# The scratch of the convolution's cells, laid out with two phases side by side

## The reference

```
x = x + L0(gn(x))     # shifted 8x8 window mixing, 16 heads
x = x + L1(gn(x))     # linear attention over two scales

qkv  = w_qkv @ x                        # 768 channels
y    = conv5x5(qkv, depthwise) ; y = conv1x1(y, 96 groups of 8)
mqkv = concat(qkv, y)                   # 64 heads of 3 x 8 channels
q, k = relu(...), relu(...) ; v with a row of ones
vk   = v k^T  (8+1 x 8 per head and image)
out  = (vk q)[:8] / (vk q)[8]           # then w_proj and a batch norm
```

## Time and profile before

| | |
|---|---|
| three runs | 2719.42, 2726.9, 2731.26 us |
| profiled execution | 2727.02 us, span 2725.0 us |
| PE, DVE, ACT, POOL busy | 94%, 75%, 57%, 39% of the span |
| mean granted clock of TensorE | 0.983 |
| DMA | 285,099 packets, 628.32 MB, mean 231 GB/s |
| stores of cells | 384 of 408 KB, landing 3.9 us after issue (median) |
| loads of raw | 192 of 816 KB, 6.3 us |

### The profile page before, as it was taken

The page is one execution under the profiler, slowest core; times in us unless marked ns, Lnnn a source line. Parts: engine busy times, 40 slices in busy tenths (PEclk is TensorE's granted clock), DMA queues, the critical chain, the costliest instruction groups (busy, mean ns, idle before and its releaser), DMA issues. The chain is left out here.

```text
span 2725.0 us, 59098 instructions
## 1 busy us (share of the span) xinstructions
PE 2559.2 (94%) x20989; PEld 2015.3 (74%) x20989; DVE 2057.2 (75%) x2947; ACT 1565.7 (57%) x2137; POOL 1062.9 (39%) x1364
## 2 busy tenths in 40 slices
PE   4999998999999999959999999999999969999997
PEld 3777776777777777748888888888888836666665
DVE  4667666788778778758888888888888758888884
ACT  4666654666656666646666666666666623434342
POOL 6300003777777768840000000000000028888886
PEclk9999999999999999979999999999999979999999
DMA  5453526888878887898888888888888667887772
GB/s 167 182 213 146 201 86 209 303 301 325 318 286 292 317 291 285 273 276 204 201 200 199 201 200 201 199 201 200 200 199 201 169 217 260 288 289 275 262 262 124
DMA packets 285099, 628.32 MB, mean 231 GB/s; under 512 B 35184, under 2 KB 232560, under 8 KB 279280
## 3 DMA queue, kind: packets, MB, share of 16 engines
q1 hardware_dynamic: 274256, 561.69, 67.3%
q0 software_dynamic: 7936, 38.80, 4.2%
q10 hardware_dynamic: 2720, 25.43, 2.5%
HBM read 328.05 MB, written 300.94 MB: 231 GB/s over the span
## 5 line engine op out<-in xcount | busy, mean ns | idle before, releaser
L1687 POOL TENSOR_TENSOR ql<-q,qh 128x1024 fp32r<-128x1024 f32 x128 | 305.9, 2420 | 1034.2 <-ACT qh L1715 1034.2
L1360 PE MATMUL c_ps<-dh,wh 128*128 128x512 f32 x1152 | 471.9, 410 | 21.4 <-DVE wl L1470 19.1
L1268 ACT ACTIVATE dh<-raw 128x1632 fp32r<-128x1632 f32 x192 | 301.2, 1569 | 281.5 <-PE c_ps L1360 261.2
L1360 PE MATMUL c_ps<-dh,wl 128*128 128x512 f32 x1152 | 453.3, 394 | 0.0
L1360 PE MATMUL c_ps<-dl,wh 128*128 128x512 f32 x1152 | 452.8, 393 | 0.0
L1475 DVE TENSOR_TENSOR dl<-raw,dh 128x1632 fp32r<-128x1632 f32 x192 | 355.7, 1853 | 66.3 <-ACT dh L1268 66.3
L950 PE MATMUL o_ps<-xh,wqh 128*128 128x512 f32 x768 | 327.1, 426 | 15.7 <-DVE xl L1028 8.1
L950 PE MATMUL o_ps<-xl,wqh 128*128 128x512 f32 x768 | 303.7, 395 | 0.0
L950 PE MATMUL o_ps<-xh,wql 128*128 128x512 f32 x768 | 301.6, 393 | 0.0
L1360 PEld LDWEIGHTS c_ps<-dh,wh 128*128 128x128 f32 x1152 | 217.4, 189 | 67.7 <-issue 19.4
L1360 PEld LDWEIGHTS c_ps<-dl,wh 128*128 128x128 f32 x1152 | 216.6, 188 | 51.6
(11 more groups left out here) (211 smaller groups left out, 5431.3 us busy)
## 6 DMA issues: line engine op xcount, KB each, us to landing
qkv_scratch<-stage SPq DMA_DIRECT2D x384, 408.0 KB, 3.9
raw<-qkv_scratch SPq DMA_DIRECT2D x192, 816.0 KB, 6.3
qr_scratch<-qs SPq DMA_DIRECT2D x128, 256.0 KB, 3.0
yq_scratch<-qy SPq DMA_DIRECT2D x64, 512.0 KB, 6.8
q<-yq_scratch SPq DMA_DIRECT2D x128, 256.0 KB, 5.5
q<-qr_scratch SPq DMA_DIRECT2D x128, 256.0 KB, 6.2
ox<-x_scratch SPq DMA_DIRECT2D x8, 4096.0 KB, 14.9
out<-ox SPq DMA_DIRECT2D x8, 4096.0 KB, 13.0
```

The lines of the kernel that those rows point to most:

```text
L1268: act.activation(dh[kind][:, :], raw[kind][:, :], ACT.Copy).then_inc(hi_ready, 1)
L1360: last = pe.matmul(c_ps[:, bank(hp, j, kind, m), :], w[hp][:, kind, part, o:o + P], cells[:, :, HALF * dy:HALF * dy + HALF * NB], start=(k ...
L1687: pool.tensor_tensor(two_of(ql, n, tp), two(n, tp), two_of(qh, n, tp).bitcast(F32), ALU.subtract)\
```

## The change

The scratch becomes (3 x 32 heads, 8 pairs of phases, 8 channels, 8 images, 2, 408). The two phases of a pair are those that one unit of projections makes together (2q and 2q + 1), so they now lie beside each other for each channel and image. A store of a tile writes 3264 contiguous bytes per channel, where it wrote 1632 bytes in each of two places. A load of raw is issued as two DMAs: a = 0 fills partitions 0 to 63 with the even phases, a = 1 partitions 64 to 127 with the odd ones, each partition with four runs of 1632 bytes. ACT waits for both (32 instead of 16 on the semaphore). The rows of raw now stand in the order of even phases, then odd ones, and the taps are written to their sorted scratch in that order (line 726), in DMAs of the same shape.

```diff
--- before.py
+++ after.py
@@ -723,7 +723,8 @@
             sp.wait_ge(K["taps_out"], 16 * QT)
             for p in range(NPH):
                 src = taps_dram.rearrange("t (h c) p n -> p c (t h) n", c=D)[p, :, :, :]
-                sp.dma_start(sorted_dram[D * p:D * p + D, :, :], src).then_inc(K["taps_sorted"], 16)
+                row = D * (NPH // 2 * (p % 2) + p // 2)
+                sp.dma_start(sorted_dram[row:row + D, :, :], src).then_inc(K["taps_sorted"], 16)
             for par in range(2):
                 for g in range(GROUPS):
                     sp.wait_ge(K["x_stored"][par][g], 16 * (B // 2))
@@ -735,7 +736,7 @@
                     def tile(n, j, stored):
                         t = TILES[j]
                         p0 = 4 * ((n // 2 + 2) % 4) + 2 * ((n + 1) % 2)
-                        sp.dma_start(qkv_dram[P * t:P * t + P, p0:p0 + 2, image(i, par), :],
+                        sp.dma_start(qkv_dram[HT * t:HT * t + HT, p0 // 2, :, image(i, par), :, :].rearrange("h c a n -> h c (a n)"),
                                      stage[:, n % 2, j, :, :, :, :].rearrange("p a k y x -> p a (k y x)"))\
                             .then_inc(stored[n % 2], 16)
 
@@ -1180,7 +1181,7 @@
         summed, s_full, s_taken = sem("summed"), sem("s_full"), sem("s_taken")
         stored = [sem(f"yq_stored{i}") for i in range(2)]
 
-        qkv_v = qkv_dram.rearrange("(k h c) p b n -> k h p c (b n)", k=3, c=D)
+        qkv_v = qkv_dram.rearrange("(k h) q c b a n -> k h a (q c) b n", k=3)
         yq_v = yq_dram.rearrange("(h d) p b n -> h p d (b n)", d=D)
 
         block = ctx.enter_context(nc.Block())
@@ -1212,8 +1213,9 @@
                 sp.wait_ge(K["qr_stored"][c], 32 * 4 * B)
 
             def load(h, j, kind):
-                sp.dma_start(raw[kind][:, :], qkv_v[kind, h, :, :, IMG * PN * j:IMG * PN * j + IMG * PN])\
-                    .then_inc(raw_loaded[kind], 16)
+                for a in range(2):
+                    sp.dma_start(raw[kind][P // 2 * a:P // 2 * a + P // 2, :].rearrange("p (b n) -> p b n", b=IMG),
+                                 qkv_v[kind, h, a, :, IMG * j:IMG * j + IMG, :]).then_inc(raw_loaded[kind], 16)
 
             def store(h, j, s):
                 own.wait_ge(q_out, s + 1)
@@ -1263,7 +1265,7 @@
             def high(s, kind):
 
                 u = 3 * s + kind
-                act.wait_ge(raw_loaded[kind], 16 * (s + 1))
+                act.wait_ge(raw_loaded[kind], 32 * (s + 1))
                 at_least(act, m_full, 3 * (u - 2))
                 act.activation(dh[kind][:, :], raw[kind][:, :], ACT.Copy).then_inc(hi_ready, 1)
 
@@ -1983,7 +1985,7 @@
     out = nc.dram_tensor("out_0", (B, C, H, W), F32, kind="ExternalOutput").ap()
     scratch = {
         "x1": nc.dram_tensor("x1_scratch", (B, C, H * W), F32, kind="Internal").ap(),
-        "qkv": nc.dram_tensor("qkv_scratch", (3 * C, NPH, B, PN), F32, kind="Internal").ap(),
+        "qkv": nc.dram_tensor("qkv_scratch", (3 * AH, NPH // 2, D, B, 2, PN), F32, kind="Internal").ap(),
         "qr": nc.dram_tensor("qr_scratch", (2 * P, NPH, B, POS), F32, kind="Internal").ap(),
         "yq": nc.dram_tensor("yq_scratch", (C, NPH, B, POS), F32, kind="Internal").ap(),
         "taps_sorted": nc.dram_tensor("tap_sorted", (P, QT * HT, TAP * TAP), F32, kind="Internal").ap(),
```

## The result

The changed kernel takes 2744.6 us, the median of six runs (2732.13 to 2753.62), where the kernel before takes 2727.1 in the same session. The ratio is 1.0068, 95% interval [1.0039, 1.0098]: 17.5 us slower. That is inside the range that was given (2714 to 2755), but 17 us above the time that was named, and it is the outcome "slower by more than 14 us", which had a chance of 0.17. Timed again, it gave 2744.6 and 1.0073 [1.0051, 1.0094].

The account below looks back on a forecast made before the run. TensorE was taken to bound projections and convolution. Span 2725.0 - 2.5 (projections) + 0 (steady convolution) + 3 (convolution start) = 2725.5 us, 2727.5 with what lies around it; named 2728, range 2714 to 2755.

Parts of the forecast that it names:

- The loads' terms: Convolution: the loads cut into short runs cost 0 us in the steady part and +3 us at the start.
- The stores' term: Projections: longer store runs relieve GpSimd's wait around the image loads, -2.5 us at TensorE, bounds 0 and -10.8.
- the prediction's own list: Signs of being wrong: steady dh waiting for DMA, the store's DMA share up, or ACT's first dh unchanged at 1205.56.
- rival 1: Steady convolution: loads become the bound above 4.61 us each; at 4.8 us +36, 2764 us; chance 0.13.
- in the direction of the store the form costs nothing: Projections' stores: a 16 x 8 DRAM side is as fast as before, as the yq store has that form.
- the 131 worked out: Projections' stores: one 3264-byte run takes 13 + 118 = 131 ns, in place of 2 x 72 = 144.
- The 161 ns of a yq run: Convolution's yq store: a 4096-byte write takes 161 ns, used as evidence that the 16 x 8 form is fast.
- the third rival: Projections: the 16 x 8 form halves the stores' rate as it does the loads', +77 us, 2805; chance 0.05.
- +3 us for the start of the convolution: First raw load: its short runs alternate with GpSimd's 4096-byte runs and land 1.5 to 4.4 us later, delaying TensorE.
- about 1208: Start of the convolution: the time in the trace, in us, at which ACT's first dh should come.
- The steady convolution: Loads of 4.13 us stay hidden behind TensorE's 15.13 us step: 0 us, DMA share 0.88 to 0.90.
- the bound from above: Convolution's loads: four 1632-byte runs take at most 477 + 39 = 516 ns, the value the prediction used.

Follow-up runs that it names:

- after: The changed kernel against the kernel before, first measurement and trace: 2744.6 us, ratio 1.0068.
- again: The changed kernel measured and traced once more, nothing altered: 2744.6 us, ratio 1.0073 against the kernel before.
- st32: Kernel before with only its stores changed, to 3264-byte runs with a 32 x 4 x 816 DRAM side: 2725.4 us, ratio 0.9992.
- st128: Kernel before with only its stores changed, to 3264-byte runs in 128 equal DRAM rows: 2722.85 us, ratio 0.9992.
- mended: The changed kernel with its stores in 128 equal DRAM rows, partitions and taps reordered to match: 2722.7 us, ratio 0.9988 against the kernel before.
- ld128: Kernel before with loads of raw as 128 equal DRAM rows, taps and weights permuted, stores unchanged: 2722.2 us, ratio 0.9985.
- ld64: Kernel before with only its loads changed, to two DMAs of 64 x 4 x 408: 2725.95 us, ratio 1.0003.
- mendedg: mended with GpSimd's two loads held until the first raw lands and DVE's second taps wait moved into the loop: 2722.4 us, ratio 0.9998.
- ld128g: ld128 with GpSimd's two loads held until the first raw lands and DVE's second taps wait moved into the loop: 2718.3 us, ratio 0.9979.
- st16: Kernel before with only the changed kernel's stores, 3264-byte runs with a 16 x 8 x 816 DRAM side: 2739.2 us, ratio 1.0043.

## Where the prediction was right, and the step that failed

**The range held, the mechanism did not.** The loads' terms came out as said. The stores' term came out with the wrong sign, and by the prediction's own list this was a sign of being wrong: the stores' share of the DMA went up (and the six stretches have 16.0 us idle, where some 10 were said). That 2744.6 lies in the range is in good part luck: its upper end of 2755 was there for the loads as the bound of the convolution (rival 1), which did not come.

**The stores' term was the step that failed.** The sum had -2.5 us for the projections, bounds 0 to -10.8, resting on "in the direction of the store the form costs nothing". The traces have +5.4 and +7.2 us there (after, again), +9.8 with the stores alone. All four traces with the 16 x 8 form have projections of 751.8 to 761.8 us, the eight others 742.2 to 746.8. The terms around it held: the run costs 133 ns in the fast form against the 131 worked out, and then the stage is 3.0 to 4.2 us shorter than in the one before (st32, st128, mended). What was missing is 28 ns a run, 48 x 28 ns = 1.3 us in a unit. Against the kernel before that is 48 x (161 - 144) ns = 0.8 us more DMA time in a unit instead of 0.6 less.

**The evidence for the step was another store.** The 161 ns of a yq run were read in 1526:1527, the microsecond in which only the rest of a store is under way. Over 1300:2100 the records of the kernel before give 182 ns on the mean, and one run in ten takes 272 or more. That is not yet the form. Two thirds of these runs start with no run of a load under way and take 162 ns on the mean; the third that has one beside it takes 224. In ld128, where the loads are 128 equal rows and the yq store is untouched, all of them have 161 ns on the mean, and 2 in 100 take over 200. So the reading was right: a yq store in the 16 x 8 form runs at full speed. What failed is the step from it to the stores of cells, which have the same form, other addresses and shorter runs, and stand in a row on the queue where a yq store stands alone. There the same form costs 28 ns a run. The prediction had one case of the form slow (the loads at 477 ns) and one fast, and took direction for the difference. Direction is not it: the stores of cells are writes too.

**It was a weak form of the third rival.** That rival had the form halve the stores' rate, for 2805 us; its sign, "the store's share of the DMA up instead of down", is what came (74.6% to 80.4%). A run took a fifth longer (161 against 133 ns), not twice as long, and of the 4.5 us that TensorE lost in 452:1187, 3.0 lie in the six stretches around the images. With a chance of 0.05 and no case between nothing and half, the chance of slower was too small. The point between was open: the loads showed half, the yq store nothing, and no row had the new stores.

**The gap.** The sum had +3 us for the start of the convolution (bounds 1.5 to 4.4). ld64, with nothing else changed, gives +2.9, mended +2.8: right in size. That the competing queue is its cause is supported by the gates: holding GpSimd's transfers back shortens the gap by 5.9 us with the loads cut in four (mended, mendedg), and by 2.4 us with loads of whole rows (ld128, ld128g). The measured gap of +6.6 has a second source that the prediction did not have: the slower stores at the end of the projections; st16, whose loads are unchanged, has +7.3. By SP's timeline it is their backlog, which holds SP's last stores (issued in 3.00 us after 0.92) and with them the loads behind. The forecast of "about 1208" for ACT's first dh came to 1212.1. The two sources do not add up: +7.3 and +2.9 alone, +6.6 and +5.5 together.

**The steady convolution.** 0 us was right, PE 910 of 910, and so, closely, were the signs: share 0.87 (0.88 to 0.90 said), a load of 64 partitions landing in 5.5 us. A 1632-byte run of these loads took 120.5 ns by the records, four of them 482 where the bound from above was 516. The Trainium skill, "SBUF — State Buffer", section on the DMA port swizzle, has 64 partitions at 196 to 218 GB/s; 6528 x 16 / 482 is 217, so the trace agrees. The first rival (loads as the bound) did not come. That the load of 128 partitions was hardly faster before was not in the load's size, though, as ld128 shows.

**What this leaves of the 17.5 us.** The stages of the two traces sum to +10.6 and +12.9 from the projections on; the medians say +17.5 (and 17.6). Runs of the changed kernel spread over 21 us, those of st16 over 4, and the two profiled runs of the changed kernel are the first and third fastest of their six (2732.1 and 2741.3 us). Stores alone +12, loads alone +1 (interval -3 to +5): 4 to 5 us are in the two together, or in the choice of traces, and I cannot tell these apart. A part of the projections' loss is the clock: in 805:835 of the changed kernel the granted clock is 0.89 on the mean,

```profile
805.00:835.00 30.00, 24.18 (x229) 18.95 (x228) 14.89 (x25) 13.87 (x20) 18.77 (x27) 0.89 0.96 338
```

after TensorE had stood idle there; the lower level (1.2 GHz) lasts 6.8 us, in the kernel before 3.4 us. Half of the difference, 1.7 us, is lost by that. It does not part the forms by itself: over the whole of the projections the lower level lasts 6.8, 13.6, 13.6 and 23.8 us in the four traces with the 16 x 8 form, and 3.4 to 10.2 us in the eight others.

**What stays open: why these transfers.** Shown is that the same bytes of the stage's stores are fast with 128 or 32 as outer dimension of the DRAM side, and slow with 16: a run takes a fifth longer. The same bytes of a load take a third longer with 16 x 8 than with 128 equal rows (456 against 337 ns on the mean). It is not shown that the outer dimension does it. The DRAM addresses, or their order, change with it in every pair of runs, and the yq store has an outer dimension of 16 and is fast when it stands alone. Nor is it shown that reads and writes suffer from one effect. Which engine touched which partitions, no trace shows. The Trainium skill, "DMA: Bandwidth & Descriptors", section on the descriptor swizzle, gives each engine, in a plain transfer of 128 partitions, the eight that share one SBUF port, which are two groups of four neighbours. If an outer dimension of 16 makes each engine take eight neighbouring partitions instead, two engines go through the same two ports in the same order, and could meet in each. The factor of two in the slow runs fits it (267 against 128 ns). Against it stands the yq store of ld128: it should meet in the same way, and its runs take 161 ns. So this is a guess that one measurement supports and one speaks against. A store of cells that stands alone, and the 16 x 8 form at other addresses, would be the next runs.

## What to carry to other kernels

A longer contiguous run is worth its fixed part (here 13 ns per run) only if the transfer keeps its rate per byte; look at the shapes and addresses of both sides after such a change, not at bytes and runs alone. In this kernel 128 equal rows were the safe choice, for stores and loads. That one transfer of a form is fast says nothing of another with other addresses and neighbours on the queue: take the mean and the slow tenth of its own runs over a whole stage, and split the runs by what runs beside them. And compare stages between traces rather than spans: here an untouched stage hid 5.5 us of a loss of 10.6.

## What the runs showed of the hardware

- The DRAM side alone (shape, and with it the addresses or their order) moved a 3264-byte write from 133 to 161 ns a run, and a 6528-byte read from 337 to 456 ns on the mean, 248 to 459 in the median; in two stretches with all engines busy, stores went at 390 against 308 GB/s.
- A 16 x 8 DRAM side is not always slow: 4096-byte writes of this form took 161 ns on the mean in ld128. Beside runs of a 16 x 8 load they took 224 ns, alone 162 (before).
- Two queues took turns run by run with 16384 against 1632 bytes and with 6528 against 4096; holding the 4096-byte queue back brought the first load 4.2 us forward, and moved the wait to DVE and to the next load.
- The gain of a lighter DMA queue was small while TensorE was the bound: in ld128 the convolution's DMA share fell from 0.83 to 0.62, and its length by 1.3 us; the traces with the loads of before differ by 2.7.
